# Four of six gathered expert rows are added by TensorE, and the gathers start among the last products

## The reference

```python
h = dA * h + dt[:, :, None] * b[:, None, :] * xt[:, :, None]
y = jnp.einsum('bdn,bn->bd', h, c)
...
a = relu2(h) * route_w[:, :, None]
routed = jnp.einsum('tei,eih->th', a, w2_experts)
return (shared + routed).reshape(orig_shape)
```

## Time and profile before

| | us |
|---|---|
| median of 3 runs | 998.32 |
| lowest, highest | 996.9, 1007.28 |
| profiled execution, its time | 1004.18 |
| profiled execution, its span | 1002.4 |
| DVE busy in the span | 898.6 (90%) |
| PE busy | 738.0 (74%) |
| POOL busy | 628.2 (63%) |
| ACT busy | 559.4 (56%) |

### The profile page before, as it was taken

One profiled execution on the slowest core, in us unless ns is written; L12 is line 12 of the kernel. 1 busy time (PEld: TensorE's weight loads), 2 busy tenths in 40 slices (PEclk: granted clock), 3 DMA queues, 4 the chain that ended last, 5 costly groups with the idle time before them and its releaser, 6 DMA issues.

```text
span 1002.4 us, 18897 instructions
## 1 busy us (share of the span) xinstructions
PE 738.0 (74%) x6728; PEld 464.8 (46%) x6728; DVE 898.6 (90%) x758; ACT 559.4 (56%) x833; POOL 628.2 (63%) x412
## 2 busy tenths in 40 slices
PE   2947664585557989998798999989889985424338
PEld 2624343152125666655565665656655652112116
DVE  7689899889989999999899999999989999999994
ACT  3553125433336878777687877788777773212220
POOL 5161558877788656665666667666656667577760
PEclk9979797676577999999899999999999995555558
DMA  9659602535549999999999999999999965263332
GB/s 329 212 182 342 206 6 88 202 114 172 175 152 243 252 283 274 281 257 268 278 285 255 289 288 297 284 265 288 257 256 290 305 193 163 77 177 100 104 94 90
DMA packets 178206, 217.32 MB, mean 217 GB/s; under 512 B 50465, under 2 KB 137378, under 8 KB 177890
## 3 DMA queue, kind: packets, MB, share of 16 engines
q1 hardware_dynamic: 168898, 190.93, 67.4%
q0 software_dynamic: 9216, 25.18, 8.0%
HBM read 144.61 MB, written 71.30 MB: 215 GB/s over the span
## 4 chain that ended last, share of the span: by engine, by line
PE 45%; DVE 27%; issue 12%; ACT 7%; SPq 4%; DMA 3%; POOL 2%; DVEq 0%; ACTq 0%; POOLq 0%
PE ps L1293 18%; DVE H L1143 8%; PE ps L1304 6%; PE ps L1390 6%; PE ps L1363 5%; DVE U L1122 4%; DVE XN L1166 3%; ACT ps L834 3%; PE ps L1371 3%; DMA WE<-w_exp_dram 2%; PE ps L1406 1%; ACT YO L891 1%; DVE H L1048 1%; SPq L429 1%; PE ps L1243 1%
## 5 line engine op out<-in xcount | busy, mean ns | idle before, releaser
L1143 DVE TENSOR_TENSOR_SCAN H<-ps,U 128x1024 f32<-128x1024 f32 x256 | 581.6, 2283 | 38.0 <-ACT ps L834 31.9
L834 ACT ACTIVATE ps<-ps,Acur 128x1024 f32<-128x1024 f32 x256 | 278.9, 1090 | 243.4 <-PE ps L1304 242.0
L639 POOL TENSOR_TENSOR U<-X,B 128x1024 f32<-128x1024 f32 x100 | 238.0, 2380 | 166.5 <-DVE H L1143 107.3
L1304 PE MATMUL ps<-PK,sel 24*128 24x512 bf16 x824 | 154.9, 440 | 176.6 <-DVE H L1143 138.7
L1293 PE MATMUL ps<-H,CB 128*32 128x128 f32 x4096 | 240.9, 395 | 5.7 <-DVE H L1143 5.7
L1293 PEld LDWEIGHTS ps<-H,CB 128*32 128x32 f32 x4096 | 143.6, 130 | 85.5 <-issue 26.5
L1304 PEld LDWEIGHTS ps<-PK,sel 24*128 24x128 bf16 x824 | 43.0, 93 | 286.0 <-issue 278.6
L639 POOL TENSOR_TENSOR U<-GS,B 128x1024 f32<-128x1024 f32 x50 | 119.5, 2390 | 20.0 <-DVE H L1143 20.0
L713 POOL DMA_INDIRECT WE<-yg_d,slot x96 | 94.2, 981 | 40.9 <-issue 21.6
L625 POOL DMA_INDIRECT xg_d<-XN,slot x96 | 95.5, 995 | 35.5 <-issue 27.6
L1363 PE MATMUL ps<-XT,WE 128*128 128x128 f32 x640 | 94.7, 296 | 6.5 <-DMA WE<-w_exp_dram 6.5
(11 more groups left out here) (172 smaller groups left out, 661.2 us busy)
## 6 DMA issues: line engine op xcount, KB each, us to landing
X<-g_d SPq DMA_DIRECT2D x200, 256.0 KB, 5.9
WE<-w_exp_dram SPq DMA_DIRECT2D x160, 256.0 KB, 4.7
xg_d<-CB SPq DMA_DIRECT2D x20, 1024.0 KB, 10.9
XG<-xg_d SPq DMA_DIRECT2D x80, 256.0 KB, 6.3
yg_d<-YO SPq DMA_DIRECT2D x80, 256.0 KB, 6.0
PK<-pk_d SPq DMA_DIRECT2D x64, 128.0 KB, 5.6
pk_d<-H SPq DMA_DIRECT2D x12, 256.0 KB, 2.8
X<-x_dram SPq DMA_DIRECT2D x4, 512.0 KB, 5.7
```

Of the source, the lines that this page charges most:

```text
L639: nc.gpsimd.tensor_tensor(U[:, c % 4, :], rows, B2[:, b * L:(b + 1) * L], ALU.mult).then_inc(u_pool, 1)
L834: nc.scalar.activation(a_tile(c), a_tile(c), ACT.Exp, scale=Acur[:, b, pair:pair + 1]).then_inc(a_ready, 1)
L1143: V.tensor_tensor_scan(H[:, (s // GRP % 2) * GRP + s % GRP, :], a_tile(s), U[:, s % 4, :], 0.0, ALU.mult, ALU.add).then_inc(scan_done, 1)
L1304: return mm(ps[:, bank, :], sel[32 * g:32 * g + ROWS, c % SUB, :], PK[32 * g:32 * g + ROWS, c // SUB % NPK, :], start=True, stop=True)
```

## The change

It has four parts, all in blocks 1 to 7:

1. Rows 0 to 3 of each row block are no longer added by DVE. ACT scales the identity matrix by the token's weight for each of them (`scale_ident`, into the buffers XT, RL and AS, which are free by then), and PE multiplies this diagonal matrix with the gathered row and sums four such products in bank 6 of PSUM (`add_row`). It does two per tile, from tile 2 on. DVE adds the sum to XN (`add_sum`).
2. Rows 4 and 5 stay with DVE, one per tile, from tile 2 on instead of four per tile from tile 9 on.
3. The first 12 gathers are issued among POOL's last 12 steps, one behind each, and the wait for all stores of expert outputs goes ahead of the first of them. Later gathers wait for the row two row blocks earlier to be used, by PE or by DVE.
4. `REST` is 14 instead of 8: the 80 pairs take places 2 to 87 instead of 2 to 92, with fewer free places among them.

Row block 15 is added after the loop: `add_row` for it stands ahead of the last `y_rows` on PE.

```diff
-COMB = 9
+COMB = 2
+ON_PE = 4
+EARLY = 12
...
-REST = 8
+REST = 14
...
+        scaled = [XT[:, u, k, :] for u in range(2) for k in range(2)] + [RL[:, 0, :], RL[:, 1, :], AS[:, 0, :], AS[:, 1, :]]
...
+        def rows_in(s):
+
+            return [((s - COMB) // 2, ON_PE // 2 * (s % 2) + k) for k in range(ON_PE // 2)] if COMB <= s < COMB + 2 * TT else []
+
+        def sums(t):
+
+            return ps[:, 6, 0:D]
+
+        def added(t, k):
+
+            return 3 * t + k - ON_PE + 1
...
+                    n = it * SL + c - (LATE - EARLY)
+                    if n == 0:
+                        for par in range(MBUF):
+                            pool.wait_ge(s_mo[par], 16 + 16 * len(range(par, NPAIR, MBUF)))
+                    if 0 <= n < EARLY:
+                        gather(n)
+
+            def gather(n):
+
+                t, k = n // TOPK, n % TOPK
+                if t >= 2 and k < ON_PE:
+                    pool.wait_ge(rows_summed, t - 1)
+                elif t >= 2:
+                    pool.wait_ge(comb, added(t - 2, k))
+                pool.indirect_dma_start(row(n), None, yg_d,
+                                        bass.IndirectOffsetOnAxis(ap=slot[:, k, t:t + 1].bitcast(u32), axis=0))\
+                    .then_inc(s_g[n % RING], 16)
...
-            for par in range(MBUF):
-                pool.wait_ge(s_mo[par], 16 + 16 * len(range(par, NPAIR, MBUF)))
-            for t in range(TT):
-                for k in range(TOPK):
-                    n = t * TOPK + k
-                    pool.wait_ge(comb, at_least_0(n - RING + 1))
...
+            for n in range(EARLY, TT * TOPK):
+                gather(n)
...
+            def scale_ident(m):
+
+                t, k = m // ON_PE, m % ON_PE
+                if m == 0:
+                    act.wait_ge(consts, 1)
+                    act.wait_ge(slots_ready, 1)
+                if t >= 2:
+                    act.wait_ge(rows_summed, t - 1)
+                nc.scalar.activation(scaled[m % len(scaled)], ident[:, :], ACT.Copy, scale=wn[:, t, k:k + 1])\
+                    .then_inc(scaled_ident, 1)
...
+                    if it == BLK - 1:
+                        for t, k in rows_in(s + 1):
+                            scale_ident(t * ON_PE + k)
...
-                    if isinstance(it, int) and it == BLK - 1 and s >= COMB:
-
-                        for n in range(TT * TOPK * (s - COMB) // (SL - COMB), TT * TOPK * (s - COMB + 1) // (SL - COMB)):
-                            combine(n)
...
+                    if it == BLK - 1:
+                        two_of_a_row_block(s)
...
+            def combine(t, k):
+
+                n = t * TOPK + k
                 dve.wait_ge(s_g[n % RING], 16 * (n // RING + 1))
-                if n:
-                    dve.wait_ge(comb, n)
+                if t == 0 and k == ON_PE:
+                    dve.wait_ge(x_again, 16)
                 else:
-                    dve.wait_ge(x_again, 16)
+                    dve.wait_ge(comb, added(t, k) - 1)
...
+            def two_of_a_row_block(s):
+
+                t = (s - COMB) // 2
+                if COMB <= s < COMB + 2 * TT:
+                    if t and s % 2 == 0:
+                        add_sum(t - 1)
+                    combine(t, ON_PE + s % 2)
+
+            def add_sum(t):
+
+                dve.wait_ge(rows_summed, t + 1)
+                dve.wait_ge(comb, 3 * t + 2)
+                V.tensor_tensor(XN[:, t, :], sums(t), XN[:, t, :], ALU.add).then_inc(comb, 1)
...
+                    if it == BLK - 1:
+                        for t, k in rows_in(s):
+                            add_row(t, k)
...
+            def add_row(t, k):
+
+                n = t * TOPK + k
+                if n == 0:
+                    pe.wait_ge(moe_out, NPAIR + 2)
+                if t and k == 0:
+                    pe.wait_ge(comb, 3 * t)
+                pe.wait_ge(scaled_ident, t * ON_PE + k + 1)
+                pe.wait_ge(s_g[n % RING], 16 * (n // RING + 1))
+                ins = mm(sums(t), scaled[(t * ON_PE + k) % len(scaled)], row(n), start=(k == 0), stop=(k == ON_PE - 1))
+                if k == ON_PE - 1:
+                    ins.then_inc(rows_summed, 1)
...
+            for s in (SL, SL + 1):
+                for t, k in rows_in(s):
+                    add_row(t, k)
             y_rows(BLK * 4 - 1, SL - GRP, 0, 16)
```

More of the change, by code:

```diff
@@ L247, in state_space_and_experts @@
         comb = sem("comb")
+        scaled_ident = sem("scaled_ident")
+        rows_summed = sem("rows_summed")
         out_ready = sem("out_ready")
@@ L705, in _ @@
             body(BLK - 1)
-            for par in range(MBUF):
-                pool.wait_ge(s_mo[par], 16 + 16 * len(range(par, NPAIR, MBUF)))
-            for t in range(TT):
-                for k in range(TOPK):
-                    n = t * TOPK + k
-                    pool.wait_ge(comb, at_least_0(n - RING + 1))
-                    pool.indirect_dma_start(row(n), None, yg_d,
-                                            bass.IndirectOffsetOnAxis(ap=slot[:, k, t:t + 1].bitcast(u32), axis=0))\
-                        .then_inc(s_g[n % RING], 16)
+            for n in range(EARLY, TT * TOPK):
+                gather(n)
         @block.scalar
@@ L899, in _ @@
             body(BLK - 1, False)
+            for t, k in rows_in(SL + 1):
+                scale_ident(t * ON_PE + k)
             evac_group(BLK * 4 - 1, 1)
@@ L1152, in body @@
                         product(it, s + ULEAD, 0)
-                    if isinstance(it, int) and it == BLK - 1 and s >= COMB:
-                        for n in range(TT * TOPK * (s - COMB) // (SL - COMB), TT * TOPK * (s - COMB + 1) // (SL - COMB)):
-                            combine(n)
-            def combine(n):
-                t, k = n // TOPK, n % TOPK
+                    if it == BLK - 1:
+                        two_of_a_row_block(s)
+            def combine(t, k):
+                n = t * TOPK + k
                 dve.wait_ge(s_g[n % RING], 16 * (n // RING + 1))
-                if n:
-                    dve.wait_ge(comb, n)
+                if t == 0 and k == ON_PE:
+                    dve.wait_ge(x_again, 16)
                 else:
-                    dve.wait_ge(x_again, 16)
+                    dve.wait_ge(comb, added(t, k) - 1)
                 V.scalar_tensor_tensor(XN[:, t, :], row(n), wn[:, t, k:k + 1], XN[:, t, :], ALU.mult, ALU.add)\
                     .then_inc(comb, 1)
+            def two_of_a_row_block(s):
[8 more added lines that the diff above has]
+                V.tensor_tensor(XN[:, t, :], sums(t), XN[:, t, :], ALU.add).then_inc(comb, 1)
             for c in range(ULEAD):
@@ L1175, in _ @@
             body(BLK - 1, False)
-            dve.wait_ge(comb, TT * TOPK)
+            for s in (SL, SL + 1):
+                two_of_a_row_block(s)
+            add_sum(TT - 1)
+            dve.wait_ge(comb, 3 * TT)
             for t in range(TT):
@@ L1414, in _ @@
                 pe.wait_ge(out_ready, at_least_0(t - 6))
+                if t == 6:
+                    pe.wait_ge(comb, 3 * TT)
                 project(t, 0)
```

## The result

| us | before | after |
|---|---|---|
| median of 20 runs each | 999.08 | 997.73 |
| lowest, highest | 995.78, 1007.28 | 983.9, 1008.35 |
| profiled execution, its span | 1002.4 | 996.9 |
| block 0 | 113.8 | 113.8 |
| blocks 1 to 6 | 529.7 | 537.3 |

The ratio is 0.9945 [0.992, 0.9971], which is 5.5 us. The medians of all runs differ by 1.4 us only. The gain is thus between 1 and 6 us, where 17 were forecast.

A forecast was written before the change was run, and what follows sets the result against it. DVE bounds the last block; DVE, PE and DMA are nearly full in blocks 1 to 6. Last block and end -18.4, pairs +1.4, total -17.0: 987.2 us for the profiled execution, 981 off the median, range 968 to 997.

The forecast's parts named there:

- the denser pairs: Blocks 1 to 6: REST 14 changes time by -4.7 to +7.5 us, depending on the clock; middle taken, +1.4.
- rival B: Blocks 1 to 6: slower through late expert weights, 4.3 us per late load; chance 0.08.
- Scans, products and halves: Last block: DVE's scans, products and two half products need 99.5 us, unchanged.
- additions 18.9: Last block, DVE: 29 single rows at 0.40 and 14 sums at 0.52, 18.9 us in place of 51.8.
- XN's reload: Start of the last block: DVE wants it at tile 2, before it lands; 0.7 us of waiting.
- (b): Last block, tiles 3 to 6: DVE's first products out of PSUM wait for PE, 3.0 us (1.3 to 5).
- the row products: Last block: TensorE's products of gathered rows, 0.44 or 0.86 us each by clock, delay DVE by 4.0 (0 to 8).
- The last sums: Tiles 29 to 31: DVE wants row block 13's sum before PE gives it; 2.3 us of waiting.
- The end: After the last scan: y_rows starts 4.5 us later, behind add_row of row block 15; everything behind it unchanged.
- The gathers: POOL, blocks 6 and 7: early gathers among products put it 3.8 us behind; cost 0 (up to 3).
- A: Last block: PE becomes the bound, staying at the lower clock; no gain, 998 us; chance 0.20.
- C: The change fails to do what it says: early gathers hold POOL or sums come late; chance 0.12.

The follow-up runs named there:

- e1: Kernel before with REST 14 instead of 8 and nothing else; 1111.2 us against 1100.9, ratio 1.0086.
- e3: Changed kernel with the last y_rows ahead of add_row for row block 15 on PE; 1088.8 us, ratio 0.9855 to the kernel before.
- e15: Changed kernel measured a third time, unaltered, beside e13 and e14; 998.2 us, 0.998 of the kernel before by the medians, ratio 0.9836.
- e10: Kernel before with REST 14 and the second layer's expert weights not loaded; 989.3 us, ratio 0.9871 to the kernel before.
- e11: Kernel before, REST 8 kept, with the second layer's expert weights not loaded; 995.0 us, ratio 0.9948 to the kernel before.
- e14: e9 with REST 14 and twelve early gathers; 991.5 us, ratio 0.9917 to the kernel before.
- e5: Changed kernel measured again, unaltered, where block 0 takes 191 to 192 us; 1085.4 us, ratio 0.9826 to the kernel before.
- e4: Changed kernel with XN's reload at tile 22 of block 6 instead of behind it; 1084.4 us, ratio 0.9817 to the kernel before.
- e12: Changed kernel with REST 10, ten early gathers, XN's reload ten tiles earlier, second load of y later; 996.6 us, ratio 0.9867 to the kernel before.
- e7: Changed kernel with the second load of y at tile 23 instead of 15 of the last block; 1092.3 us, ratio 0.9847 to the kernel before.
- e9: Changed kernel with REST 8, six early gathers, additions from tile 4 on, last y_rows ahead of the last row products; 987.5 us against 1000.8, ratio 0.987.
- e8: Changed kernel with the edits of e2, e3, e4 and e7 together; 1086.3 us, ratio 0.9817 to the kernel before.
- e13: e9 with the second load of y at tile 23; 979.0 us against 999.8 for the kernel before, ratio 0.9811.
- e2: Changed kernel with REST back at 8 and six early gathers instead of twelve; 1082.5 us, ratio 0.9827 to the kernel before.
- e6: e2 measured again, beside e5; 1085.7 us, ratio 0.9801 to the kernel before.

## Why the prediction was wrong, step by step

The profiled execution was to lose 17.0 us and lost 5.5. Of the 11.5 between, 6.2 are the pairs, 5.8 the last block and -0.3 the end (the rest is rounding).

**The step that failed: the denser pairs, taken at +1.4.** Measured: +7.6 in the profile, +9.5 us by e1 alone. Over all traces with full weights, `REST` 14 gives 536.7 on average (eight, 527.5 to 544.8) and `REST` 8 525.9 (six, 521.6 to 529.7): +10.8, beyond the +7.5 that was the upper end. (Without e3 and e15, whose profiled executions the ratios leave out, `REST` 14 has 534.2: +8.3.)

I had asked only whom the lower clock belongs to, the free places or the stretches without one. That question has an answer, and in my favour: with half the weights loaded (e10, e11) the dense order gains 6.2, close to the -4.7 reckoned. But the share of DMA time stood at 1.00 in the earlier trace rows, and the sum carried no term for it. Its price stood in the prediction as rival B, 4.3 us for each stretch with late weights, with a chance of 0.08 and as a case of its own. It should have been a term: three more such stretches came, and a shade less than B's price each, (24.81 + 24.21 + 24.96 + 26.21 + 25.41) / 5 - 21.33 = 3.8. With the -4.7 this gives 3 x 3.8 - 4.7 = +6.7 of the 7.6. "Rates of 293 in a stretch at 21.22" was no argument against it: it says what one stretch can do, and not what happens when a load in a long row of pairs is late.

That late weights are the cause is shown by e1, e10, e11 and e14 together: the order alone costs time with all the bytes, and gains with fewer. The changed kernel's trace shows the way: each of its five long stretches holds a wait of PE for weights (1.5 to 3.6 us in sum) and one of DVE for a spread. And the traces agree among themselves. PE's wait for weights against the length of blocks 1 to 6, in us:

| kernels | PE's wait | blocks 1 to 6 |
|---|---|---|
| `REST` 8, six traces | 1.4 to 7.2 | 521.6 to 529.7 |
| e5 | 12.7 | 527.5 |
| changed, e4, e1, e14 | 15.7, 16.6, 16.8, 18.8 | 537.3, 531.7, 532.7, 531.4 |
| e12 (`REST` 10) | 17.8 | 537.6 |
| e15, e7, e3 | 21.3, 21.9, 22.8 | 544.8, 544.6, 543.3 |

Late rows of g, the obvious rival, are ruled out as the way: scans waited for POOL for at most 3.7 us in any of these traces. Not shown is that the free places let the transfers catch up; it is how I read it, but both late stretches of before hold a free place (the one at 472.35 is in the earlier trace rows). Why weights are late so much more often in one execution of the same kernel than in another is open. It would also explain why the changed kernel's times spread over 24 us where those of before spread over 12.

**The last block: 128.4 forecast, 134.2 measured, 151.3 before.**
- Scans, products and halves 99.5, additions 18.9: right. What follows a single addition starts 0.38 to 0.41 behind it, and behind a sum 0.51 to 0.53; the 0.58 of dependent additions, which went into the range, did not come.
- XN's reload: 0.7 forecast, 2.54 measured. It went out at 834.65, 0.05 us into the block instead of 0.61 ahead of it, and its wait ended 10.3 us later instead of 9.1. But e4 shows that it cost nothing of its own, since the addition behind it was held up by another cause to about the same point.
- That cause was not foreseen: additions beside POOL's last products took 1.68 and 1.41, 2.1 us above two of 0.48. The changed kernel's rows of POOL for the same moments:

```profile
843.99 2.35 POOL L657 TENSOR_TENSOR U<-GS,B 128x1024 f32<-128x1024 f32 x1
...
847.51 2.36 POOL L657 TENSOR_TENSOR U<-X,B 128x1024 f32<-128x1024 f32 x1
```

  Products end at 846.34 and 849.87, the additions at 846.62 and 850.16, 0.3 us behind each. In all ten traces with such additions, seventeen of them, it is the same 0.3. In e9, whose first addition comes after POOL's product, it takes 0.48. The Trainium skill (SBUF — State Buffer, "Who interferes with whom") states that a DVE instruction with two inputs in SBUF and a GpSimd instruction that reads SBUF exclude one another. The rows agree but for one: the size here is the rest of the product plus 0.3 us, and the addition of e4 was held over a whole product that began behind it. Before the change no addition stood beside a POOL product: the last product ended at 837.21, and the first addition began at 859.11.
- PE's waits, (b) and the row products together: 7.0 forecast, nine waits of 3.5 in all measured, and one of 0.3 that the profile gives to nobody. The clock rose to 0.71 from 0.52, so both levels came, as taken. The products took more than their 0.44 and 0.86 (0.57 and 1.04), and the waits were still half of what was reckoned.
- A late gathered row: 3.84, not forecast. The loads of y, 1.8 MB, go out at 895.3, and gathers issued beside them land up to 9.4 us after their issue, where the median is 2.8. Moving one of the two loads removes the wait: none of over 1.5 us is left there in the four traces with this edit (e7, e8, e12, e13), and in e13 the last block is 126.9, in e9 129.9. The nine traces of the new form with both loads together have one of 2.4 to 4.3 each. In the kernel before, gathers beside these loads took up to 9.2 as well, and no addition waited: a gather was issued 14.1 us ahead of its addition there (median), and is 5.7 ahead in the changed kernel. The wait is thus a price of the change itself.

The changed kernel's SP queue, and a window behind the loads of y (columns as in the earlier trace rows):

```profile
834.65 0.62 SPq L578 DMA_DIRECT2D XN<-xs_d  x1
...
895.34 0.59 SPq L551 DMA_DIRECT2D X<-ys_d  x1
895.97 0.43 SPq L552 DMA_DIRECT2D X<-ys_d  x1
```
```profile
900.00:903.00 3.00, 1.99 (x8) 0.93 (x8) 3.00 (x4) 1.19 (x3) 2.14 (x3) 0.69 1.07 292
```

- The last sums: 2.3 forecast, 2.29 measured.
- 1.3 us stay unassigned: 1.8 + 2.1 + 3.8 - 3.2 = 4.5 of the 5.8.

**The end.** y_rows 4.5 us behind the last scan forecast, 4.3 measured; the end is 4.2 longer. Right, and for the reason given: row block 15's rows arrive last. Putting y_rows first (e3, e9) doesn't shorten the end, because the row products then stand behind it on PE (4.3 us of them in e9, at the end that starts two tiles later).

**The gathers.** Cost 0 forecast; tile 2 did not wait for its row with twelve early ones, and with six (e2, e6, e8) it waited 5.5 to 8.3 us. POOL was late for a scan for 3.4 us in the whole execution, 3.2 before.

**The rivals.** A, PE as the bound of the last block, did not come: DVE waited 3.5 us for it outside the tail. It forecast the right time, 998, and that was luck: of its causes only the pairs' term was true. B came in part, its late weights but not its slower kernel. C did not come. The chances, as listed one by one, add up to 1.03, and the last line's to 1.00; nothing hangs on it.

## What to carry to other kernels

Where the share of DMA time is 1.00, an order of work that is denser for the engines needs a term for late transfers, sized by the stretches in which they are late already. Work moved to an earlier place meets new neighbours: a wait that ends there can be replaced at once by another engine's instruction or a burst of transfers, and removing the wait alone then gives nothing. When a change is several edits, run the one whose sign was a guess by itself; here it was +9.5 us, against -12.9 in the profile for the rest.

## What the runs showed that I had not expected

- A DVE addition of 128x256 f32 with both inputs in SBUF, 0.48 us alone, took 1.41 to 3.38 beside a GpSimd product of 2.35 and ended 0.3 us behind it (the changed kernel, e4, e5).
- Gathers on GpSimd's queue, 2.8 us from issue to landing in the median, took up to 9.4 while two loads from SP's queue, 1.8 MB together, were under way.
- The kernel before took 999 to 1001 us beside some of the kernels and 1101 to 1107 beside others, and both on one chip at different times. The difference lies in block 0 (191 against 114) and in the last block (179.7 against 151.3 in the old form, 149 against 134 in the new), and blocks 1 to 6 are alike. PE then stands between two instructions without a wait for anything that the profile shows, while GpSimd issues indirect transfers. From e1, PE, DVE and POOL:

```profile
930.48 0.61 PE L1304 MATMUL ps<-PK,sel 24*128 24x512 bf16 x2 [9.89 <-issue]
```
```profile
929.15 1.23 DVE L1122 TENSOR_TENSOR U<-ps,B 128x1024 f32<-128x1024 f32 x1 [9.61 <-remote]
```
```profile
928.23 0.94 POOL L713 DMA_INDIRECT WE<-yg_d,slot  x1 [0.30 <-issue]
```

  In this form the change gains 1.7% (e5: 0.9826) instead of 0.5%, since its last block loses 15 us to these stops and the old one 28. What PE stands for there was not settled; that its instructions are loaded late beside the gathers was only argued.
